# Exponentials of the cumulative sums from memory instead of from the matrix engine, and a state product placed earlier, in a Mamba-2 layer on one core

## The reference, cut to what matters

```
zxbcdt = xn @ in_proj_w.T                      # gate z, x, B, C, dt
x, B, C = silu(causal_conv4(x, B, C) + conv_b)
dt  = softplus(dt + dt_bias);  Adt = -exp(A_log) * dt
Y_diag = (C B^T * exp(segment_sum(Adt))) (x * dt)      # inside a chunk
Y_off  = C state * exp(A_cumsum)                       # from the chunks before
y = (Y_diag + Y_off + D * x) * silu(z)
out = groupnorm(y) * norm_w @ out_proj_w.T
```

## Time and profile before

| | us |
|---|---|
| three runs: median (lowest to highest) | 2206.22 (2197.03 to 2206.24) |
| the profiled execution | 2204.8 |
| its span | 2203.1 |
| PE busy, of the span | 2061.4 (94%) |
| DVE busy | 1593.6 (72%) |
| ACT busy | 964.0 (44%) |
| POOL busy | 465.2 (21%) |
| granted TensorE clock, mean | 0.973 |
| DMA engines busy | 19.8% |

### The profile page before, as it was taken

The page is one execution under the profiler, slowest core; times in us unless marked ns, Lnnn a source line. Parts: engine busy times, 40 slices in busy tenths (PEclk is TensorE's granted clock), DMA queues, the critical chain, the costliest instruction groups (busy, mean ns, idle before and its releaser), DMA issues.

```text
span 2203.1 us, 26984 instructions
## 1 busy us (share of the span) xinstructions
PE 2061.4 (94%) x10056; PEld 1383.9 (63%) x10056; DVE 1593.6 (72%) x2303; ACT 964.0 (44%) x1290; POOL 465.2 (21%) x385
## 2 busy tenths in 40 slices
PE   6799957999999999999999999999999999999987
PEld 4344425676767676766676666666666666666654
DVE  6443423586868686868687868798887879797965
ACT  2100003655555545454545445454544545455531
POOL 1100023222222222222222222222121222222200
PEclk9799988999999999999999999999999999999998
DMA  5000003213131312121212231211212121212110
GB/s 196 29 15 0 1 19 100 59 35 104 35 104 35 99 40 94 44 94 45 87 46 91 57 114 48 81 57 59 75 59 80 54 80 54 85 54 80 54 44 20
DMA packets 67361, 139.14 MB, mean 63 GB/s; under 512 B 11280, under 2 KB 16528, under 8 KB 66720
## 3 DMA queue, kind: packets, MB, share of 16 engines
q1 hardware_dynamic: 67232, 137.42, 19.4%
HBM read 127.69 MB, written 9.70 MB: 62 GB/s over the span
## 4 chain that ended last, share of the span: by engine, by line
PE 66%; issue 6%; DVE 6%; ACT 5%; DMA 2%; POOL 1%; SPq 0%; POOLq 0%; ACTq 0%; DVEq 0%
PE bank L710 31%; PE bank L809 18%; PE bank L726 4%; PE bank L739 3%; PE bank L761 3%; DVE conv L1046 2%; PE bank L768 2%; ACT wos L926 2%; PE bank L751 2%; DVE conv L1050 2%; DMA wxs<-wp 2%; ACT L906 1%; ACT conv L877 1%; PE bank L792 1%; ACT M L906 1%
## 5 line engine op out<-in xcount | busy, mean ns | idle before, releaser
L710 PE MATMUL bank<-xnp,wxp 128*128 128x512 f32 x3456 | 883.7, 408 | 43.5 <-POOLq L1018 30.0
L710 PEld LDWEIGHTS bank<-xnp,wxp 128*128 128x128 f32 x3456 | 650.8, 192 | 199.5 <-POOLq L1018 30.9
L981 POOL TENSOR_TENSOR wxp<-wxs,wxp 128x512 fp32r<-128x512 f32 x288 | 392.4, 1367 | 1097.8 <-ACT wxp L870 1097.7
L809 PE MATMUL bank<-wos,gT 128*128 128x512 f32 x1024 | 453.2, 596 | 2.6 <-DVE gT L1126 2.6
L1046 DVE SCALAR_TENSOR_TENSOR conv<-bank,cws,conv 128x509 f32<-128x509 f32 (+2 forms) x480 | 357.9, 746 | 31.1 <-ACT conv L877 19.8
L809 PEld LDWEIGHTS bank<-wos,gT 128*128 128x128 f32 x1024 | 191.0, 192 | 218.9 <-issue 215.9
L877 ACT ACTIVATE conv<-bank,cbs,cws 128x512 f32<-128x512 f32 x160 | 123.9, 775 | 310.3 <-PE bank L710 310.3
L870 ACT ACTIVATE wxp<-wxs 128x512 fp32r<-128x512 f32 x288 | 179.2, 622 | 62.4 <-DMA wxs<-wp 44.9
L1153 DVE SCALAR_TENSOR_TENSOR M<-M,gb 128x1024 f32<-128x1024 f32 x128 | 176.4, 1378 | 7.5 <-DVE gb L1145 0.5
L901 ACT ACTIVATE xT<-conv 128x512 f32<-128x512 f32 x160 | 100.1, 625 | 186.4 <-DVE conv L1050 110.2
L885 ACT ACTIVATE gT<-bank 128x512 f32<-128x512 f32 x128 | 76.3, 596 | 224.2 <-PE bank L710 223.5
(11 more groups left out here) (133 smaller groups left out, 2128.1 us busy)
## 6 DMA issues: line engine op xcount, KB each, us to landing
wxs<-wp SPq DMA_DIRECT2D x288, 256.0 KB, 2.7
wos<-wout SPq DMA_DIRECT2D x64, 512.0 KB, 5.3
state_scratch<-S SPq DMA_DIRECT2D x8, 512.0 KB, 2.9
S<-state_scratch SPq DMA_DIRECT2D x8, 512.0 KB, 3.6
w1s<-w SPq DMA_DIRECT2D x1, 3584.0 KB, 14.3
w2s<-w SPq DMA_DIRECT2D x2, 1792.0 KB, 20.7
out<-acc SPq DMA_DIRECT2D x8, 256.0 KB, 3.2
tab_scratch<-tabs SPq DMA_DIRECT2D x2, 768.0 KB, 4.8
```

The costliest lines, as they stand in the source:

```text
L710: last = pe.matmul(bank(k), wxp[:, k % 2, a, kk, :], xnp[:, half, b, kk, :], start=kk == 0 and a + b == 0, stop=kk == KT - 1 and a == 1)
L809: last = pe.matmul(Y[:, 512:512 + HID], gT[u % 2][:, t, tokens(q)], wos[:, t, :], start=t == 0, stop=t == XT - 1)
L981: pool.tensor_tensor(wxp[:, k % 2, 1], wxs[:, k % 2], wxp[:, k % 2, 0], ALU.subtract).then_inc(w_lo, 1)
```

## The change

The spread, its matrix and its exponential are gone. The prologue takes the exponential of all the sums at once on ACT (into `v`, free by then) and SP writes it to a new array `ecs_dram`, 512 KB in float32. In the scan SP loads, for every cell, the 16 heads of its group over 128 partitions: two DMAs, one for the even heads to partitions 0 to 63 and one for the odd ones to 64 to 127, each of which repeats a row of 128 tokens (512 B) for the 64 channels of a head. `ecs` has two buffers; the load for cell q+2 stands at the end of cell q in SP's list. `load_row` moves behind the last tile load of the cell. On PE `from_state` moves from behind the fourth projection to ahead of `segment_b`.

```
--- prologue
             sp.wait_ge(s_ecs, 1)
+            sp.dma_start(ecs_dram, v[:].rearrange("p t h -> p (t h)")).then_inc(s_spill, 16)
...
-            pool.wait_ge(s_csT, 2)
+            pool.wait_ge(s_ecs, 1)
...
+            act.wait_ge(s_csT, 2)
+            act.activation(v[:].rearrange("p t h -> p (t h)"), csT[:].rearrange("p t c -> p (t c)"),
+                           ACT.Exp).then_inc(s_ecs, 1)
--- scan, SP
+            def load_ecs(q):
+                if q < CELLS:
+                    _, half, g, c = place(q)
+                    t0 = (half * CH + c) * P
+                    sp.wait_ge(u1_d, done(q - 1))
+                    for e in range(2):
+                        rows = ecs_dram[g * HG:(g + 1) * HG, t0:t0 + P].rearrange("(t e) i -> e t i", e=2)[e]
+                        sp.dma_start(ecs[e * HD:(e + 1) * HD, q % 2], bc(rows, 0, [HD, XT, P])).then_inc(d_ecs[q % 2], 16)
...
             load_row(0)
+            load_ecs(0)
+            load_ecs(1)
             load_out(0)
...
                 for i, k in enumerate(tiles_of(q)):
-                    if i == 3:
-                        load_row(q + 2)
                     load_tile(k + 2)
-                if not tiles_of(q):
-                    load_row(q + 2)
+                load_row(q + 2)
+                load_ecs(q + 2)
--- scan, PE
-            def spread(q):
...
                 if more:
                     segment_a(q + 1)
-                    spread(q + 1)
                 for k in ks[2:3]:
                     project(k)
                 if more:
+                    from_state(q + 1)
                     segment_b(q + 1)
                 for k in ks[3:4]:
                     project(k)
                 if more:
-                    from_state(q + 1)
                     gram(q + 1)
--- scan, ACT
                     exp_a(q + 1)
-                    exp_c(q + 1)
--- scan, POOL
-            pool.memset(pick[:], 0.0).then_inc(built, 1)
...
-                pool.affine_select(out=pick[:], in_=pick[:], compare_op=ALU.not_equal, fill=1.0, base=-PAIRS - m * HG,
-                                   pattern=[[-2, XT], [-1, 2], [0, HD]], channel_multiplier=1).then_inc(stage, 1)
--- scan, DVE
                 dve.wait_ge(yo_mm, done(q + 1))
-                dve.wait_ge(e_c, done(q + 1))
+                dve.wait_ge(d_ecs[q % 2], 32 * (q // 2 + 1))
```

More of the change, by code:

```diff
@@ L285, in tables @@
                 if half:
-                    act.wait_ge(s_spill, 16 * (1 + half))
+                    act.wait_ge(s_spill, 16 * (2 + half))
                 for k, src in ((1, av), (2, tot)):
@@ L368, in tables @@
                 if half:
-                    dve.wait_ge(s_spill, 16 * (1 + half))
+                    dve.wait_ge(s_spill, 16 * (2 + half))
                 dve.wait_ge(s_tab, 4 * half + 2)
@@ L503, in scan @@
 def scan(nc, sb, sem, banks, wxs, d_w, xnp, acc, ident, upper, epsc, wp, wout, cws, cbs, nws, dch, d_const,
-         cs_dram, tab_dram, rest_dram, state_dram, out):
+         cs_dram, ecs_dram, tab_dram, rest_dram, state_dram, out):
     with ExitStack() as ctx:
@@ L520, in scan @@
         xdec = sb(ctx, "xdec", [P, GC])
-        ecs = sb(ctx, "ecs", [P, GC])
+        ecs = sb(ctx, "ecs", [P, 2, XT, P])
         ya = sb(ctx, "ya", [P, XT, P])
@@ L533, in scan @@
         d_out, d_acc_in = sem("d_out"), sem("d_acc_in")
+        d_ecs = [sem(f"d_ecs{p}") for p in range(2)]
         d_tab = [sem(f"d_tab{p}") for p in range(2)]
@@ L696, in _ @@
         def _(pe):
-            for s in (t_mm, yo_mm, st_mm, xt_mm, yd_mm, ec_mm, sa_mm, sb_mm, g_mm, o_mm, q_mm):
+            for s in (t_mm, yo_mm, st_mm, xt_mm, yd_mm, sa_mm, sb_mm, g_mm, o_mm, q_mm):
                 pe.sem_inc(s, CREDIT)
@@ L723, in from_state @@
                     pe.wait_ge(s_add, done(q))
-                pe.wait_ge(e_c, done(q + 1))
+                pe.wait_ge(x_dt, done(q + 1))
+                pe.wait_ge(x_dec, done(q + 1))
                 for t in range(XT):
@@ L746, in turn_x @@
                 pe.wait_ge(u1_d, done(q))
-                pe.wait_ge(e_c, done(q))
+                pe.wait_ge(x_dec, done(q))
                 if c == 0:
@@ L784, in segment_b @@
                 segment(q, 1)
-            def spread(q):
-                u, _, _, c = place(q)
-                pe.wait_ge(x_dt, done(q + 1))
-                pe.wait_ge(x_dec, done(q + 1))
-                for t in range(XT):
-                    last = pe.matmul(Z[:, t * P:(t + 1) * P], pick[:, t, :], segl[:, u % 2, c], start=True, stop=True)
-                last.then_inc(ec_mm, 1)
             def gram(q):
@@ L825, in _ @@
                     segment_b(0)
-                if k == 16:
-                    spread(0)
                 project(k)
@@ L861, in _ @@
         def _(act):
-            for s in (w_hi, tap_d, silu_d, z_d, e_a, e_b, e_c, y_sq, wo_n):
+            for s in (w_hi, tap_d, silu_d, z_d, e_a, e_b, y_sq, wo_n):
                 act.sem_inc(s, CREDIT)
@@ L910, in exp_b @@
                 act.activation(M[:, HG // 2:].rearrange("p h t -> p (h t)"), X[:], ACT.Exp).then_inc(e_b, 1)
-            def exp_c(q):
-                act.wait_ge(ec_mm, done(q + 1))
-                act.wait_ge(u1_d, done(q))
-                act.activation(ecs[:], Z[:], ACT.Exp).then_inc(e_c, 1)
             def square(q):
```

36 lines of the change are left out of this document (19 added, 17 removed).

## The result

The changed kernel takes 2229.96 us (median of 4 runs, 2226.34 to 2233.14) against 2205.46 us for the one before in the same rounds: ratio 1.0119, 95% interval 1.0090 to 1.0149. It is 1.2% slower; I had forecast 2150. The profiled span went from 2203.1 to 2227.2 us, the mean granted clock from 0.973 to 0.966.

What follows compares the result with a forecast made beforehand. PE was taken as the bound in ordinary cells, with a chain through a tile load and ACT at unit starts. Terms -17.6 - 26.7 - 5.5 - 4.4 + 4.3 - 5 = -54.9 against 2204.8 gave 2150 us; range 2136 to 2190.

Steps and rivals of the forecast that it cites:

- What one load of ecs costs: DMA queue, each cell: 512 KB as 1024 packets takes 2.5 us, lower end 1.6, upper end 6.5.
- The 4.0 us of room at the unit starts: DMA queue ahead of the output weights: 4.0 us are free, so a 2.5 us ecs load delays nothing.
- rival C: Unit starts: broadcast reads are slow, output weights and third tile queue behind ecs; 2254 us, chance 0.08.
- Rival A: Second half of the scan: DVE becomes the bound and nothing is won in its units; 2180 us, chance 0.13.
- Spread and exponential, -17.6: Cells on PE: dropping the spread wins 0.45 us in each of 39 cells, -17.6 us.
- Product moved, -26.7: 15 unit starts: the product with the state fills PE's wait for ACT, 1.78 us each, -26.7 us.
- clock, -5: Unit starts: PE's shorter wait brings back half of the 9.7 us lost to the lower clock, -5 us.
- The last cells, -5.5: Last three cells: the product with the state runs while ACT works, so the gram comes earlier, -5.5 us.
- POOL's constants, -4.4: Start of the scan: PE and SP wait less for POOL, as one memset and three selects go, -4.4 us.
- The loads at the start of the scan, +4.3: Start of the scan: four ecs loads (1.05 MB) ahead of output weights and third tile cost +4.3 us.
- What the move delays: PE, ACT and DVE in each cell: second half of differences comes 1.3 us later, costed at nothing; without cover 18 us.
- queue positions: SP's list: the row goes out some 5 us later in five-tile cells, SP waits for nothing new; costed at nothing.

Runs made afterwards that it cites:

- 4 KB run: Changed kernel with the ecs array laid out so the eight rows of a load lie side by side as one 4 KB run: 2145.91 us, ratio 0.9742.
- padded version: Changed kernel with 512 B of padding behind each head's row in memory, so a load's eight rows lie 9 KB apart: 2144.40 us, ratio 0.9733.

## Why the prediction was wrong, step by step

The forecast missed by 80 us because of one step, *What one load of ecs costs*. All other terms moved the time the way that was forecast; some gave more and some less, as told below.

- **The failed step.** I took 2.5 us per cell from a store with as many packets, and set its upper end at 6.5 from the earlier trace rows. Engine time was indeed 2.2 us, but in the changed kernel the two loads of a cell trickle over 6.8 us, and one lands 8.9 us after its issue. A price per packet from engine time was the wrong measure: the engines were mostly not busy while the next transfers waited. Distinct rows (4.2 us), a 4 KB run (4.1), 576 B (4.5) and 9 KB (4.4) take away one property each; what is left as the cause is the two together, eight rows 8 KB apart and each read by 64 partitions. The number of partitions that read a row was never varied.
- **The 4.0 us of room at the unit starts.** The estimate of where it hurts was right, and I had worked out 7.3 us per cell as the break-even in rival C. The loads went past it: +36.0 us at the unit starts, where the padded version has -33. They cost 5.0 us per start (70 us in 14), which with the 4.0 us of room is a price of some 9 us per cell, near the 9.6 with which rival C was worked out. Rival C's place (weights and third tile behind ecs) was the one; its mechanism was half right, since with rows side by side or 9 KB apart the repeats cost nothing. It also said nothing of SP, whose next four issues are held up: 3.14 us at 641.35 and 11.63 at the scan's start, against the 1.75 of the earlier trace rows.
- **Rival A** played a part of a few us. In the second half an ordinary interval is 0.5 us shorter only in one of three per unit; in the other two the saving is about zero, and the waits for DVE's convolution have grown. They are as long with the move undone (14.0 us in 23 places), so it isn't the move. For the padded version, a row of PE's waits; before it read 3.9 us in 8 places:

```profile
PE bank L726 <- DVE conv L1045: 13.7, 23, 1.0
```

- **Spread and exponential, -17.6.** Measured -14.8: 21 intervals of the first half at 0.51 (I took 0.45) and in the second half 7 instead of the 14 I had counted, 4.0 us.
- **Product moved, -26.7, and clock, -5.** With padded rows the unit starts take 420.2 us instead of 453.1: -33 for 14, where the terms for 15 give -31.7, or -29.6 for 14. A start with a fast tile went from 31.5 to 29.8 us in the first half and from 31.8 to 30.05 in the second, 1.8 each, just the product's 1.78: 25 us. The rest is the clock, less 1.5 us, most of it at unit 8. I gave back half of its 9.7 us; with padded rows no fourth tile at a unit start was slow any more, so all of it came back. (Most other versions with fast loads kept one slow tile, at unit 8; it took 4.40 us in the 4 KB version.) Undoing the move brought the waits of 2.3 to 2.7 us and six slow tiles back together.
- **The last cells, -5.5.** Measured -9.2. It comes from the move: undone, the last four take 85.7 us, no less than the 83.4 of before. I had counted only the wait for the exponential, and not what the earlier product lets run behind it; which operation gives the rest I didn't separate.
- **POOL's constants, -4.4.** Measured -4.3 (30.02 to 25.73).
- **The loads at the start of the scan, +4.3.** With these and POOL's the start should have been even; it was 11.0 us later. Counted from PE's first projection, so that POOL's part and the prologue's own 4 us of difference between traces are out, the first output product comes after 91.9 us before, 107.1 in the changed kernel (+15.2), 96.5 with padding and 96.8 with a 4 KB run (+4.6 and +4.9). With fast loads +4.3 was right; the failed step is what made it 15.2. Moving the four loads away takes 6.2 us off again (padded) or 8.7 (4 KB run).
- **What the move delays, queue positions:** no sign of either in the ordinary cells of any version. Around the change of halves three intervals got 0.9 to 2.7 us longer in the versions with fast loads, which I had not forecast and didn't trace further.

So the sum without the failed term comes out: the padded version, the same change with 512 B more per row, takes 2144.40 us, and its profiled span is 2144.1, 59 us shorter than before where I had 55. That it is so close is in part luck: too little for the clock and the last cells (some 8 us) stands against too much for the spread and nothing for the change of halves (some 5), and the prologue of that trace happens to end 4 us sooner. The effect of the loads alone was shown on both sides: on the kernel before (2278.50 against 2202.49, +76 us) and by padding (2229.96 to 2144.40, -86 us). Why 8 KB and 64 repeats together are slow isn't settled by these runs. They show it is a matter of which addresses are read at once; what lies behind it in the memory, none of them shows.

## What to carry to other kernels

A load that repeats a few short rows for many partitions should be priced by its landing time in a run of its own, not by bytes, packets or engine time; lay the rows side by side or pad them, since a distance of 8 KB doubled the landing here and turned a gain of 2.7% into a loss of 1.2%. On a shared queue a slow load costs whoever stands behind it, and it shows in other rows than its own (the weights' landing, SP's issue time, PE's wait for a tile). Where a queue has to begin with something, begin with what the chain waits for first: with the first ecs loads behind the tiles, the first cell's output product came 6 to 9 us sooner after PE's first projection, though the whole time moved by only 1 to 6 us, hardly more than these runs can tell.

## What the runs showed of the hardware

- Eight rows of 512 B read by 64 partitions each, by distance of the rows, median us to landing of 256 KB: side by side 4.1, 576 B 4.5, 4 KB 5.7, 8 KB 8.9, 8 KB and 128 B 6.1, 9 KB 4.4. With 512 distinct rows 8 KB apart: 4.1.
- The Trainium skill, "DMA: Bandwidth & Descriptors", section "Latency and other measured facts", has a row on pitches at large powers of two: 207 GB/s at 512 KiB per partition and 103 at 4 MiB, where a padding of 4 KiB restores the rate and 192 B doesn't. The runs agree in kind, since a power-of-two distance is slow and enough padding cures it, but at a distance 64 times smaller than the page's smallest and only where rows are repeated; and here 128 B more between the rows already gave back some three fifths.
- The same skill's page "SBUF — State Buffer", section "Door 1: The DMA port swizzle", gives 196 GB/s for a load of 1 MiB on 64 partitions (about 218 for large ones), and, in the section "Can I just issue two DMAs to hit both halves?" behind it, only 6% more for two on the two halves at once. With distinct rows the slices of the two loads reach 200 to 309 GB/s, some 250 in the mean of the 2 us: this doesn't contradict a limit for one load alone, but for the pair the measurement decides, and no cost of the halves showed.
- Issuing costs time when loads are slow: the four issues of output weights took 1.75 to 1.79 us at unit starts before, 1.76 in the padded version, and 2.13 to 7.19 us at the 14 unit starts of the changed kernel.
- A wait of 2.69 us of PE was followed by a fourth tile of 5.68 us, one of 0.91 us by 3.16. The granted clock was 0.50 behind the first and 1.00 behind the second. Not every longer wait is followed by a slow tile: at the 14 unit starts of the table, behind waits of 2.17 to 2.69 us, six were slow in the kernel before and six with the move undone; behind waits of 0.53 to 1.43 us in the changed and the padded kernel none was.
